# Layer 2 of a four-layer graph network: mask and row maximum in one pass of eight tensor_tensor_reduce per graph

## The reference

```python
scores = jnp.einsum('bhnd,bhmd->bhnm', q, k) / math.sqrt(D)
mask = adjacency[:, None, :, :] == 0
scores = jnp.where(mask, -jnp.inf, scores)
w = jax.nn.softmax(scores, axis=-1)
out = jnp.einsum('bhnm,bhmd->bhnd', w, v)
out = out.transpose(0, 2, 1, 3).reshape(b, n, e)
return out @ Wo.T + bo
```

## Time and profile before

| | |
|---|---|
| median of 3 runs | 769.99 us (769.66 to 771.23) |
| profiled execution | 769.41 us, its span 767.7 us |
| PE, PE weight loads | 677.0 us (88%), 510.2 us (66%) busy |
| DVE, ACT, POOL | 610.3 us (80%), 545.4 us (71%), 448.4 us (58%) busy |
| chain that ended last | PE 53%, DVE 20%, issue 10%, ACT 9%, POOL 4% |
| granted PE clock, mean | 0.966 |

### The profile page before, as it was taken

One profiled execution on the slowest core, in us unless ns is written; L12 is line 12 of the kernel. 1 busy time (PEld: TensorE's weight loads), 2 busy tenths in 40 slices (PEclk: granted clock), 3 DMA queues, 4 the chain that ended last, 5 costly groups with the idle time before them and its releaser, 6 DMA issues.

```text
span 767.7 us, 17876 instructions
## 1 busy us (share of the span) xinstructions
PE 677.0 (88%) x6525; PEld 510.2 (66%) x6525; DVE 610.3 (80%) x1562; ACT 545.4 (71%) x949; POOL 448.4 (58%) x486
## 2 busy tenths in 40 slices
PE   3999599999669999999999998789999999999973
PEld 2787477777535666666666666667777777777752
DVE  3699568888847788888888887598888888888882
ACT  0555277777727877787777776388888888888882
POOL 5387413343335456656766666176777667776685
PEclk9999899999958999999999999899999999999996
DMA  8900000000000000000000000000000000000001
GB/s 229 272 2 1 1 1 1 2 1 2 1 0 1 2 1 2 2 1 2 2 2 2 2 1 2 1 2 1 16 15 22 24 15 17 15 22 23 15 15 42
DMA packets 28888, 14.94 MB, mean 19 GB/s; under 512 B 1920, under 2 KB 28800, under 8 KB 28800
## 3 DMA queue, kind: packets, MB, share of 16 engines
q1 hardware_dynamic: 25344, 12.59, 5.9%
q10 hardware_dynamic: 3456, 1.20, 0.7%
HBM read 9.59 MB, written 4.19 MB: 18 GB/s over the span
## 4 chain that ended last, share of the span: by engine, by line
PE 53%; DVE 20%; issue 10%; ACT 9%; POOL 4%; POOLq 2%; DMA 1%; DVEq 1%; ACTq 0%
PE pair L963 19%; PE pair L1091 5%; PE quad L1060 4%; ACT loopm L691 3%; PE pair L1152 3%; DVE arena L941 3%; DVE nmx L947 3%; PE pair L1071 3%; PE pair L1065 2%; PE pair L1029 2%; DVE bn L537 2%; DVE z L861 2%; PE pair L1077 2%; PE quad L1023 2%; POOL arena L608 2%
## 5 line engine op out<-in xcount | busy, mean ns | idle before, releaser
L594 POOL TENSOR_TENSOR arena<-arena,nmx 128x1024 f32<-128x1024 f32 x64 | 121.3, 1895 | 90.3 <-DVE nmx L887 88.6
L608 POOL TENSOR_TENSOR arena<-arena,nmx 128x1024 f32<-128x1024 f32 x64 | 121.3, 1895 | 81.3 <-DVE nmx L947 81.3
L963 PE MATMUL pair<-identf,arena 128*128 128x128 f32 x1088 | 151.6, 281 | 0.5 <-ACT arena L785 0.5
L506 POOL TENSOR_TENSOR ln<-ln,neghalf 128x4 f32<-128x4 f32 x64 | 66.1, 1033 | 131.1 <-DVE ln L546 131.1
L963 PEld LDWEIGHTS pair<-identf,arena 128*128 128x128 f32 x1088 | 117.7, 142 | 31.4 <-issue 30.3
L512 POOL TENSOR_SCALAR X<-yb,ln 128x128 f32<-128x128 f32 x256 | 111.8, 449 | 11.9 <-issue 11.9
L772 ACT ACTIVATE arena<-quad 128x1024 f32<-128x1024 f32 x64 | 66.1, 1033 | 31.2 <-PE quad L1142 31.2
L880 DVE TENSOR_TENSOR arena<-quad,mask 128x1024 f32<-128x1024 f32 x64 | 77.7, 1215 | 5.2 <-PE quad L1060 4.5
L887 DVE TENSOR_REDUCE nmx<-arena 128x8 f32<-128x1024 f32 x64 | 78.0, 1218 | 1.8
L947 DVE TENSOR_REDUCE nmx<-arena 128x8 f32<-128x1024 f32 x64 | 78.0, 1218 | 1.7
L941 DVE TENSOR_TENSOR arena<-quad,arena 128x1024 f32<-128x1024 f32 x64 | 77.6, 1212 | 0.2 <-issue 0.2
(11 more groups left out here) (193 smaller groups left out, 1447.8 us busy)
## 6 DMA issues: line engine op xcount, KB each, us to landing
X<-in_x SPq DMA_DIRECT2D x16, 256.0 KB, 6.1
arena<-in_adj SPq DMA_DIRECT2D x16, 256.0 KB, 6.6
out<-X SPq DMA_DIRECT2D x16, 256.0 KB, 2.3
nat_all<-in_L_gnn_W ACTq DMA_DIRECT2D x2, 64.0 KB, 4.8
w<-in_L_gnn_W ACTq DMA_DIRECT2D x2, 64.0 KB, 5.5
nat_all<-in_L_gnn_W_loop ACTq DMA_DIRECT2D x1, 64.0 KB, 2.7
nat_all<-in_L_gnn_Wg_loop ACTq DMA_DIRECT2D x1, 64.0 KB, 3.3
hg_bias<-in_L_gnn_b_loop ACTq DMA_DIRECT2D x1, 64.0 KB, 5.0
```

The lines of the kernel that those rows point to most:

```text
L594: nc.gpsimd.tensor_tensor(v3(P2[t % 3], HEADS), v3(P2[t % 3], HEADS), nmx2[t % 2][:].unsqueeze(2).broadcast_to([128, HEADS, N]), ALU.add)\
L608: nc.gpsimd.tensor_tensor(v3(p, HEADS), v3(p, HEADS), nmx2[(t - 1) % 2][:].unsqueeze(2).broadcast_to([128, HEADS, N]), ALU.add)\
L963: last = nc.tensor.transpose(dst[:, cols(i)], src[:, cols(i)], identf[:])
```

## The change

DVE no longer adds the mask to the whole tile and then reduces it. For each of the 8 heads one `tensor_tensor_reduce` reads 128 scores from PSUM and the 128 mask values from SBUF, writes their sum to P2 and the largest of them (from a start value of -3e38) to a column of nmx2. L2_masked is signalled after the eighth, and stands for both results; L2_max is no longer used. The maximum is not negated any more, so POOL subtracts. The wait for POOL (L2_less_max) that stood before the reduction stands before the first head.

```diff
+LOWEST = -3e38
...
             def layer2(t):
                 if graph(t):
-                    pool.wait_ge(sem("L2_max"), t + 1)
+                    pool.wait_ge(sem("L2_masked"), t + 1)
                     nc.gpsimd.tensor_tensor(v3(P2[t % 3], HEADS), v3(P2[t % 3], HEADS),
-                                            nmx2[t % 2][:].unsqueeze(2).broadcast_to([128, HEADS, N]), ALU.add)\
+                                            nmx2[t % 2][:].unsqueeze(2).broadcast_to([128, HEADS, N]), ALU.subtract)\
                       .then_inc(sem("L2_less_max"), 1)
...
                     dve.wait_ge(sem("L2_s_mm"), t + 1)
                     need(dve, sem("L2_pT_mm"), t - 2)
-                    nc.vector.tensor_tensor(p, s, mask2[:, cols(t)].unsqueeze(1).unsqueeze(1).broadcast_to([128, 4, 2, N]), ALU.add)\
-                      .then_inc(sem("L2_masked"), 1)
+                    need(dve, sem("L2_less_max"), t - 1)
+                    for h in range(HEADS):
+                        last = nc.vector.tensor_tensor_reduce(p[:, h // 2, h % 2], s[:, h // 2, h % 2], mask2[:, cols(t)], 1.0, LOWEST,
+                                                              ALU.add, ALU.max, nmx2[t % 2][:, h:h + 1])
+                    last.then_inc(sem("L2_masked"), 1)
                 if j == 2 and real(b - 3):
                     stats_done(dve, 2, (b - 3) % 2)
-                if graph(t):
-                    dve.wait_ge(sem("L2_masked"), t + 1)
-                    need(dve, sem("L2_less_max"), t - 1)
-                    nc.vector.tensor_reduce(nmx2[t % 2][:], v3(P2[t % 3], HEADS), AX.X, ALU.max, negate=True)\
-                      .then_inc(sem("L2_max"), 1)
```

## The result

The changed kernel takes 774.02 us (median of 6 runs, 773.12 to 775.11) where the kernel before, run beside it, takes 771.43 (6 runs, 769.66 to 771.79). The ratio is 1.0039, 95% interval 1.0025 to 1.0053: slower by 0.4%. The profiled execution took 773.12 us with a span of 771.4, against 769.41 and 767.7: 3.7 us of span to explain.

What follows compares the result with a forecast made beforehand. PE was taken to set the pace, busy 15.34 of 15.80 us per four graphs. Start 1.73 plus steady 0.2 gave 1.9 us on 769.41, so 771.3, and 0.58 for the median: 771.9 us; range 769.8 to 787.

Steps and rivals of the forecast that it cites:

- DVE's price: DVE in layer 2: eight new two-instruction passes per graph take 2.30 us, replacing two passes of 2.39 us.
- data part: First instruction of each new DVE pass, handling the 128 elements; priced at 0.203 us, upper end 0.262.
- reading part: Second instruction of each new DVE pass, writing the 128x1 maximum; priced at 0.085 us, between nothing and 0.095.
- T: DVE time per graph for the eight new passes in layer 2; 2.30 us, between 1.62 and 2.86.
- cheap reading: Rival: writing the maxima costs DVE nothing, 1.62 us per graph; +0.49 us at layer 2's start, 770.5 us; chance 0.12.
- the case without overlap: Rival: each DVE instruction waits for the previous one's end, 3.8 us per graph; DVE becomes the bound, 827 us; chance 0.09.
- The steady release: Layer 2's steady periods: PSUM quad handed back to PE 0.015 us late in graph 0, 13 batches; 0.2 us.
- The start: Start of layer 2, where PE waits for the mask: +1.165 us in graph 0, +0.565 in graph 1; +1.73.
- the half-absorbed rival: Rival: PE's clock rises at the same moment despite the late layer 2 start, leaving 1.07 us, 771.1; chance 0.20.
- The other edits: Layer 2: POOL's earlier start, subtract for add, the moved POOL wait and 896 more DVE instructions; all priced at nothing.
- What would show it: Signs expected in the changed profile: pairs 0.29 us apart, PE's wait 4.3 us, period 15.8, DVE busy time nearly unchanged.

Runs made afterwards that it cites:

- e1: Changed kernel, but in graph 2 of a batch POOL's subtraction waits until DVE has finished the batch statistics; 769.72 us, ratio 0.999 to the kernel before.
- e4: Kernel before, but PE's next scores wait for the row maximum (L2_max) instead of the mask pass (L2_masked); 781.05 us, ratio 1.013.
- e5: Changed kernel, with the first of the two small tensor_scalars of layer 2's statistics written as a tensor_reduce; 772.79 us, ratio 1.0023 to the kernel before.
- e2: Changed kernel, with the end of the statistics moved ahead of the eight heads at graph 2; 771.74 us, ratio 1.0015 to the kernel before.
- e3: Kernel before, with the end of the statistics moved behind the row maximum at graph 2, no new instruction; 782.2 us, ratio 1.0153.

## Why the prediction was right, and where its reasons were not

The forecast, slower at 771.9 us against 769.99, was right in sign; against the 771.43 measured beside it, the kernel lost 2.6 us where I had 1.9. The range holds it. The steps, one by one:

- **DVE's price.** I had 0.288 us for a pair, and pairs start 0.21 apart. My 0.203 for the data part, from L820's row less its elements, is nearly all of that, so the reading part, priced at 0.085, was wrong: the next data part starts with it, and by my estimate for the data part it adds about 0.01 (no run has a data part alone). T is 1.69, not 2.30, near the end that I called cheap reading. The Trainium skill's 258 ns for the data part ("VectorE: DVE Perf Modes", errata section) is near the part's length (0.28) but is not borne out as a spacing: 8 x 0.258 = 2.06 for the 1.69 measured. The page's section "The DRAIN you can't avoid" in the Trainium skill, which I cited for the case without overlap, also says that a next op that is not held starts earlier. The rows agree with that part: each next pair starts 0.07 us before the last data part ends.
- **The steady release.** Priced at 0.2, for graph 0 alone. With T = 1.69 it is nothing: e1's period is 15.80. In e4 graph 0's next scores come 0.1 us later than before, so the room I read there was real.
- **The start.** +1.73 with T = 2.30; with 1.69 the same working gives 0.56 (1.69 + 0.135 - 1.27, and graph 1 fits), and PE did resume 0.58 later. To the first yb +0.3 was left of it in e1 and -0.1 in the changed kernel, whose clock had risen earlier: the half-absorbed rival's mechanism, on a smaller sum. e4, with the release I had assumed, gave +1.9 to +2.0.
- **"The other edits", the step that failed.** I wrote that L2_masked comes "before the statistics instead of behind them in graph 2", concluded that "nothing is gained there", and priced it at nothing. That is where the 3.0 us of the periods come from. I asked what POOL's earlier start could bring to ACT, not what it would run beside. DVE's L545 and L546 stood in the rows, at 0.17 each, and the rule that would have made me ask was in the Trainium skill. I did not weigh it. The trace of the kernel before even holds one such standstill, in layer 3, which I overlooked (timeline; POOL's second subtraction ends at 509.99):

```profile
506.24 3.75 POOL L608 TENSOR_TENSOR arena<-arena,nmx 128x1024 f32<-128x1024 f32 x2
...
508.03 1.99 DVE L545 TENSOR_SCALAR ln<-mv 128x4 f32<-128x4 f32 x1
```

- **What would show it.** Of the signs, POOL's wait on the new line came true, and so did the length of the data part (0.28). The spacing (0.29), the wait (4.3 us for the measured 3.70), DVE's busy time "nearly unchanged" (13.87 became 12.84) and "the period still 15.8" did not. A period of 16.06 was none of my cases.

So the sign was right by luck, for another reason than mine: the loss that I priced is at most some 0.5 us, under what can be told here, and the cause of the measured loss was not in the prediction. The likeliest outcome by my own terms, with T right, would have been cheap reading (770.5, no change), and e1, which is that kernel, measures so.

What stays open is the last period of layer 2, 2.1 us longer in the changed kernel. Here it is in e1, e5 and e2 (windows, columns as above):

```profile
460.27:474.91 14.64, 12.81 (x156) 9.50 (x157) 11.48 (x85) 9.51 (x13) 10.29 (x10) 1.00 0.01 3
461.82:477.21 15.39, 12.81 (x156) 9.51 (x157) 12.24 (x84) 9.52 (x13) 10.16 (x10) 1.00 0.01 2
459.59:476.45 16.86, 14.33 (x156) 10.82 (x157) 11.57 (x84) 9.62 (x13) 11.73 (x12) 0.90 0.01 2
```

e5 has a standstill there (1.01 us, on its tensor_scalar) and takes 15.39 us, 0.4 more than the kernel before and 0.75 more than e1. e2 has none and takes 16.86, with PE busy 1.5 us longer at a granted clock of 0.90. The changed kernel, e3 and e4 also show 0.90 or 0.91 there and take 17.07, 18.03 and 17.67; all others show 1.00 and take 14.6 to 15.4. So most of the 2.1 goes with the clock, which is at its lower level (1.2 GHz) for part of that period, and less than half with the standstill. Why the clock falls there in four of ten profiles is not shown, nor whether it would in another execution of the same kernel. That the clock rose earlier at the start of layer 2 in the changed kernel was seen in one profile, too.

The best version found is e1: the new pass with POOL held in graph 2. Its interval (0.998 to 1.0001) lies below the changed kernel's (1.0025 to 1.0053) and can't be told from the kernel before.

## What to carry to other kernels

When a change lets an engine start earlier, list what it will now run beside, and look whether the two share anything: an instruction that stands still for another engine can look busy, not waiting. So compare the mean ns of the same group before and after, and look at a group's longest instruction already in the trace before: L545's was 1.99 us where its median was 0.17. Here a shortened pass on an engine with slack brought nothing (e1), and lost by moving its neighbours. The order of two small steps (statistics, then maximum) can be worth 12 us of 770 by what it keeps apart, and one semaphore wait (e1) can keep them apart just as well.

## What was unexpected of the hardware

- A tensor_scalar over 128x4 fp32 values in SBUF took 1.46 us instead of 0.17 beside a 1.90 us GpSimd tensor_tensor, in 12 of 12 statistics of 250 to 460 us, while bn_aggr (0.38), a tensor_reduce of the same size (0.16) and DVE's reciprocal from PSUM (0.20 to 0.21) kept their times.
- A tensor_tensor_reduce of 128 fp32 elements from PSUM and a mask in SBUF is two instructions, 0.28 and 0.08 us long, and costs 0.21 us in a row of eight.
- What a late start of a stage cost went with the moment at which the clock rose: 0.58 us more of wait cost -0.1 and +0.3 us to the first yb in two profiles (clock 0.66 and 0.50 in 232 to 234). And the stretch ahead of layer 2, the same in all ten kernels, took 222.1 to 224.5 us.
